# Decoder layer on one core: bf16 operands in the router's one-hot comparisons, and the softmax's subtraction of the maximum on VectorE instead of GpSimd

## What is computed

```
logits = einsum('bhqd,bhkd->bhqk', q, k) * scale
logits = logits + mask[:, None, None, :] * -1e9
attn = softmax(logits)                 # maximum subtracted, exp, divided by the sum
...
vals, idx = top_k(y @ gate_w.T, 2)
w = softmax(vals)
out = sum over the two experts e of a row:  w * W3[e](silu(W1[e] y) * (W2[e] y))
```

## Time and profile before

| what | value |
|---|---|
| three timed runs | 1579.9, 1581.67, 1582.06 us (median 1581.67) |
| the profiled execution | 1582.67 us |
| its span | 1580.8 us, so 1.87 us lie around it |
| mean granted clock of TensorE | 0.966 of 2.4 GHz |
| PE / DVE / ACT / POOL busy | 1420.2 / 1045.0 / 927.3 / 648.9 us |

### The profile page before, as it was taken

One profiled execution on the slowest core, in us unless ns is written; L12 is line 12 of the kernel. 1 busy time (PEld: TensorE's weight loads), 2 busy tenths in 40 slices (PEclk: granted clock), 3 DMA queues, 4 the chain that ended last, 5 costly groups with the idle time before them and its releaser, 6 DMA issues. The chain is left out here.

```text
span 1580.8 us, 23151 instructions
## 1 busy us (share of the span) xinstructions
PE 1420.2 (90%) x7425; PEld 902.6 (57%) x7426; DVE 1045.0 (66%) x1406; ACT 927.3 (59%) x646; POOL 648.9 (41%) x484
## 2 busy tenths in 40 slices
PE   6899999999999999999998569999984799999995
PEld 4555555555555555554554157777764566676664
DVE  7878998889888988898887726666665322222221
ACT  1879888988998899889989602222221122222221
POOL 5255456545554555455543512212220233333331
PEclk9899999999999999999999879999995899999998
DMA  4000000000000000000000313111120134233312
GB/s 145 14 1 15 27 27 13 13 27 27 13 13 27 27 13 13 27 27 13 7 14 14 113 40 109 44 42 53 46 81 14 22 87 139 35 82 81 88 30 70
DMA packets 67483, 66.90 MB, mean 42 GB/s; under 512 B 5152, under 2 KB 59936, under 8 KB 67424
## 3 DMA queue, kind: packets, MB, share of 16 engines
q1 hardware_dynamic: 60160, 56.58, 11.0%
q0 software_dynamic: 7296, 9.97, 3.8%
HBM read 48.70 MB, written 19.92 MB: 43 GB/s over the span
## 5 line engine op out<-in xcount | busy, mean ns | idle before, releaser
L1630 POOL TENSOR_TENSOR v_aug<-v_aug,wts 128x1024 f32<-128x1024 f32 x96 | 254.8, 2654 | 250.1 <-ACT wts L1483 245.5
L998 DVE TENSOR_SCALAR wts<-ps_s,k 128x1024 f32<-128x1024 f32 x240 | 297.2, 1280 | 85.4 <-PE ps_s L538 64.5
L1475 ACT ACTIVATE wts<-wts 128x4096 f32<-128x4096 f32 (+1 forms) x80 | 231.8, 2935 | 88.5 <-DVE wts L998 68.8
L553 PE MATMUL ps_o<-wts,g_r 128*64 128x512 f32 x1024 | 251.4, 614 | 11.3 <-ACT wts L1483 11.2
L1481 ACT ACTIVATE wts<-wts,eps_d 128x4096 f32<-128x4096 f32 (+1 forms) x80 | 241.5, 3019 | 0.2
L1483 ACT ACTIVATE wts<-wts 128x4096 f32<-128x4096 f32 (+1 forms) x80 | 235.1, 2939 | 2.5
L1396 DVE TENSOR_TENSOR wts<-rinv,ps_s 128x352 f32<-128x352 f32 x76 | 39.6, 521 | 253.7 <-ACT rinv L1548 170.6
L793 PE MATMUL ps_s<-wts,qk 128*128 x608 | 197.9, 469 | 3.1 <-issue 2.3
L987 DVE TENSOR_TENSOR v_aug<-v_aug,wts 128x1024 f32<-128x1024 f32 x96 | 156.1, 1626 | 5.4 <-ACT wts L1483 5.1
L538 PE MATMUL ps_s<-q_hi,k_hi 64*128 64x512 f32 x512 | 115.8, 446 | 40.3 <-DVE wts L998 30.1
L793 PEld LDWEIGHTS ps_s<-wts,qk 128*128 128x128 f32 x608 | 110.6, 192 | 64.6 <-issue 16.8
(11 more groups left out here) (240 smaller groups left out, 2425.2 us busy)
## 6 DMA issues: line engine op xcount, KB each, us to landing
wts<-in_w SPq DMA_DIRECT2D x16, 704.0 KB, 5.4
h_t<-o_raw SPq DMA_DIRECT2D x16, 512.0 KB, 2.6
qk<-h_t SPq DMA_DIRECT2D x16, 512.0 KB, 4.1
wts<-in_w SPq DMA_DIRECT2D x8, 640.0 KB, 7.1
raw_qk<-in_w_in SPq DMA_DIRECT2D x32, 128.0 KB, 2.2
raw_vg<-in_w_in SPq DMA_DIRECT2D x32, 128.0 KB, 2.2
acc<-wts SPq DMA_DIRECT2D x17, 128.0 KB, 1.7
wts<-in_x SPq DMA_DIRECT2D x2, 1024.0 KB, 6.0
```

The source lines that it names most:

```text
L553: mm = pe.matmul(ps_o[r, t], v_pair[:, b, r], wts[:, h, b, t], start=b == 0, stop=b == SB - 1)
L998: dve.tensor_scalar(wts[:, h, b, :], ps_s[:, h, :], k2[:, 2 * b + h:2 * b + h + 1], 0.0, ALU.add, ALU.max).then_inc(S_.max_ok, 1)
L1475: act.activation(chunk(start, end), chunk(start, end), ACT.Sqrt).then_inc(S_.sqrt_ok, 1)
L1630: pool.tensor_tensor(acc_w[:, 0], acc_w[:, 0], wts[:, 0, b], ALU.add).then_inc(S_.add_ok, 1)
```

## The change

The router's constants and slot numbers become bf16 (three copies of constants are made at the end of step 16 on VectorE), and the subtraction moves from GpSimd's step into VectorE's `mask_max`, behind the reduction:

```diff
-        hl_f = take(4 * NT)
+        hl_f = take(2 * NT).bitcast(BF16)
+        rb = take((P + ET + NT) // 2).bitcast(BF16)
+        pos_b, tile_b, tok_b = rb[:, 0:P], rb[:, P:P + ET], rb[:, P + ET:P + ET + NT]
@@ VectorE, mask_max
-                if n >= 1:
-                    dve.wait_ge(S_.sub_ok, i)
                 dve.tensor_reduce(lmax[:], lg, AX.X, ALU.max).then_inc(S_.lmax_ok, 1)
+                dve.wait_ge(S_.lmax_ok, i + 1)
+                dve.tensor_tensor(lg, lg, lmax[:].unsqueeze(2).broadcast_to([P, XH, KC]), ALU.subtract).then_inc(S_.sub_ok, 1)
@@ VectorE, at the end of step 16
                     dve.tensor_copy(sums, rc[:, R_TRI:R_ONES + P])
+                    dve.tensor_copy(pos_b, rc[:, R_POS:R_POS + P])
+                    dve.tensor_copy(tile_b, rc[:, R_TILE:R_TILE + ET])
+                    dve.tensor_copy(tok_b, rc[:, R_TOK:R_TOK + NT]).then_inc(S_.rb_ok, 1)
@@ VectorE, router
+            dve.wait_ge(S_.rb_ok, 1)
             dve.wait_ge(S_.hl_ok, 2)
-                q = dve.tensor_tensor(oh_hi[k][:, :, 0], rc[:, R_TILE:R_TILE + ET]...
+                q = dve.tensor_tensor(oh_hi[k][:, :, 0], tile_b...
-                dve.tensor_tensor(oh_lo[k], rc[:, R_POS:R_POS + P]...
+                dve.tensor_tensor(oh_lo[k], pos_b...
-                                  rc[:, R_TOK:R_TOK + NT].unsqueeze(2).broadcast_to([P, NT, ET]), ALU.mult)
+                                  tok_b.unsqueeze(2).broadcast_to([P, NT, ET]), ALU.mult)
@@ VectorE, weigh_slots
-                dve.tensor_tensor(one_hot, rc[:, R_TILE:R_TILE + ET]...
+                dve.tensor_tensor(one_hot, tile_b...
@@ GpSimd, step
-                if s2:
-                    pool.wait_ge(S_.lmax_ok, t)
-                    pool.tensor_tensor(lg, lg, lmax[:].unsqueeze(2).broadcast_to([P, XH, KC]), ALU.subtract).then_inc(S_.sub_ok, 1)
```

More of the change, by code:

```diff
@@ L249, in program @@
         tok_now = sb("tok_now", [P, 2], U32)
-        names = ("x_in", "xb_in", "cst_in", "c_in", "fill_s", "fill_ok", "xnb_ok", "max8_ok", "at_ok", "stats_ok", "aggr_ok", "std_ok", "rstd_ok", "xn_ok", "tr_ok", "xnt_ok",
+        names = ("x_in", "xb_in", "cst_in", "c_in", "fill_s", "fill_ok", "xnb_ok", "rb_ok", "max8_ok", "at_ok", "stats_ok", "aggr_ok", "std_ok", "rstd_ok", "xn_ok", "tr_ok", "xnt_ok",
                  "qk_in", "vg_in", "wqk_ok", "wvg_ok", "xh_ok", "x2_in", "q_proj", "k_proj", "v_proj", "g_proj", "norm_mm", "k2_mm",
@@ L260, in program @@
                  "pta_ok", "lr1", "r1_ok", "lr2", "r2_ok", "ms_ok", "lr3", "r3_ok", "exp_ok",
-                 "x1b_ok", "sub_ok", "base_ok", "top_ok", "topi_ok", "topf_ok", "dlt_ok", "pe_ok", "pw_ok", "wf_ok",
+                 "x1b_ok", "sub_ok", "base_ok", "top_ok", "topf_ok", "dlt_ok", "pe_ok", "pw_ok", "wf_ok",
                  "rc_in", "oh_ok", "a_ok", "rank_mm", "rt_ok", "tab_ok", "slot_ok", "hl_ok", "oh2_ok", "tok_mm", "tok_ok",
@@ L1328, in _ @@
             dve.tensor_copy(hl_f, hl_i[:]).then_inc(S_.hl_ok, 1)
+            dve.wait_ge(S_.rb_ok, 1)
             dve.wait_ge(S_.hl_ok, 2)
             for k in range(2):
-                q = dve.tensor_tensor(oh_hi[k][:, :, 0], rc[:, R_TILE:R_TILE + ET].unsqueeze(1).broadcast_to([P, NT, ET]),
+                q = dve.tensor_tensor(oh_hi[k][:, :, 0], tile_b.unsqueeze(1).broadcast_to([P, NT, ET]),
                                       hl_f[:, k * NT:(k + 1) * NT].unsqueeze(2).broadcast_to([P, NT, ET]), ALU.is_equal)
@@ L1334, in _ @@
             for k in range(2):
-                dve.tensor_tensor(oh_lo[k], rc[:, R_POS:R_POS + P].unsqueeze(1).broadcast_to([P, NT, P]),
+                dve.tensor_tensor(oh_lo[k], pos_b.unsqueeze(1).broadcast_to([P, NT, P]),
                                   hl_f[:, (2 + k) * NT:(3 + k) * NT].unsqueeze(2).broadcast_to([P, NT, P]), ALU.is_equal)
@@ L1364, in weigh_slots @@
                 one_hot = oh_w[k][:, 0]
-                dve.tensor_tensor(one_hot, rc[:, R_TILE:R_TILE + ET].unsqueeze(1).broadcast_to([P, NT, ET]),
+                dve.tensor_tensor(one_hot, tile_b.unsqueeze(1).broadcast_to([P, NT, ET]),
                                   hl_f[:, k * NT:(k + 1) * NT].unsqueeze(2).broadcast_to([P, NT, ET]),
@@ L1674, in _, with step @@
             pool.wait_ge(S_.c_in, C_IN)
-            def step(t, s1=True, s2=True, s4=True):
+            def step(t, s1=True, s4=True):
                 if s4:
@@ L1690, in _ @@
             for t in range(4):
-                step(t, s2=t >= 1, s4=t >= 3)
+                step(t, s4=t >= 3)
             with pool.Fori(4, NT) as t:
@@ L1694, in _ @@
             for t in range(NT, NT + 3):
-                step(t, s1=False, s2=t <= NT)
+                step(t, s1=False)
             def fetch(k, par, n):
```

## The result

The changed kernel takes 1.0151 times the time before, 95% interval [1.0129, 1.0173]. On 1581.67 us that is about 1605.6 us, where 1594.9 was forecast and 1598 was the upper end of the range. The direction was right, the size was not. Six runs lie between 1599.37 and 1630.97 us (median 1609.03), those of the kernel before beside them between 1576.57 and 1586.14: the new kernel also scatters further, by 31.6 us against 9.6, and by 11.6 without its two slowest. (Ratios here are of runs at most 1.5% above the fastest of their kernel; medians and ranges in the text are of all runs.) The profiled execution took 1603.76 us, its span is 1601.5, 20.7 longer than before.

What follows compares the result with a forecast made beforehand. It took a loop ring of VectorE (reduction to group 1's copy), then TensorE to the logits, as the bound. Terms 11.55 + 1.31 + 0.57 + 0 - 0.85 + 0.62 = 13.2 us on 1581.67 gave 1594.9 us; range 1590 to 1598 (its own 1592 to 1598).

Steps and rivals of the forecast that it cites:

- The ring: Tile loop: VectorE from the reduction to the copy of group 1, then TensorE to the logits, sets the 16.67 us period.
- VectorE's price: Subtraction in the tile loop: 1.44 us on VectorE, with the division starting 2.84 us after the reduction instead of 1.79.
- copies and comparisons: Router constants' three casts, at the end of VectorE's step 16, and its bf16 comparisons: both costed at nothing.
- 11 x 1.05 = 11.55: Steps 5 to 15 of the tile loop: division delayed by 1.05 us in each, 11.55 us in all.
- the 1.31 of step 4: Tile loop, step 4: the division follows the reduction without a wait, so it is delayed by 1.31 us.
- TensorE falls to its lower clock in the loop: Rival: about 1 us more idle ahead of `turn_o` halves the loop's clock, some 100 us, 1695 us in all; chance 0.02.
- the prediction's own signs of being wrong: Loop period staying at 16.7 us, L1335 near 1.2 us, or the loop's clock under 1.00.
- Step 1: First loop step, no division: TensorE waits 4.56 us for the exponential, which comes sooner; a gain of 0.85 us.
- Step 2: Second loop step: division 2.84 us after the reduction instead of 2.27, a loss of 0.57 us.
- Step 3: Third loop step: TensorE's 0.73 us wait for the DMA covers the delay; taken as 0, bound 0.57 us.
- Step 16: Last subtraction: VectorE delayed 1.48 us, the transposes follow `x_out`; path delayed by 0.62 us, bound 1.48.
- the rival with 3.5 us: Router: bf16 comparisons run faster, saving 3.5 us ahead of TensorE's L775, total 1591.4 us; chance 0.12.

Runs made afterwards that it cites:

- e1: The changed kernel with three extra matmuls of constants on TensorE ahead of `turn_o` in every step, against the kernel before: ratio 1.0161, median 1621.32 us.
- A alone filled: Same run as `e1`: of TensorE's three idles per step in the changed kernel, only the 1.03 us ahead of `turn_o` filled with extra matmuls; ratio 1.0161.
- f12: The kernel before (subtraction on GpSimd) with `best_two` one step later, ahead of the mask, and `h_t` loaded in two halves: ratio 0.9891, median 1564.71 us.

## Why the prediction missed

- **The ring and VectorE's price: right.** Subtraction 1.44 us, division 2.83 us after the reduction (2.84), step of 17.61 us (17.7), TensorE's idle ahead of `turn_o` 1.03 us (1), copies and comparisons worth nothing. The term "11 x 1.05 = 11.55" and the 1.31 of step 4, 12.86 together, measure 11.2 at full clock: from the copy of group 1 to the mask it is 6.92 us instead of 7.02, all of it between the start of the logits and the mask (2.75 instead of 2.85; why isn't seen), so a usual step loses 17.61 - 16.69 = 0.92 us.
- **The clock in the loop: the step that failed.** It stood as a rival, "TensorE falls to its lower clock in the loop", with the right cause (about 1 us more idle ahead of `turn_o`), but priced as all or nothing, "some 100 us in all", and so held for nearly impossible (0.02); only for step 16 did I count an earlier fall at a limited price, "1 to 2 us". The clock comes and goes within single steps, which costs 0.2 to 1.7 us in ten of twelve, 8.7 us in all in this trace, and up to 2.9 us a step in others. Without it the profiled kernel would have been 20.7 - 8.7 = 12.0 us slower, 1593.7 us on the median, inside "1592 to 1598". Its model of a fall was the tail, which stays at 0.50. The row to weigh was that of step 1 (933.07:949.30, above), with a clock of 0.89 and an idle of 4.56 us in it: a fall that lasts for part of a step. A clock under 1.00 in the loop was one of the prediction's own signs of being wrong.
- **Step 1: wrong by 0.83.** The exponential does start earlier, by 0.86 us, but the clock of this stretch went from 0.89 to 0.79, and its period stayed 16.21. In `e1`, the same program up to there, the clock was 1.00 and the period 13.72, so the clock weighed more here than the term.
- **Step 2: +0.26 instead of +0.57.** `turn_x` comes 0.54 us later, but the output projection behind it had waited about 0.2 us for `h_t`, and this wait took up the difference.
- **Step 3: +0.15**, with a clock of 0.90 where it was 1.00.
- **Step 16: -0.07 instead of +0.62.** Group 0 and 1 do start 1.59 us later (6.67 us after the reduction, against 5.08 in the earlier trace rows), but the clock comes back during them: groups 2 and 3 take 0.64 and 0.66 us instead of 1.97 together.
- **The comparisons: right**, against the rival with 3.5 us. With one operand broadcast along the innermost dimension the bf16 form takes as long as the f32 form (2284 ns against 2287 for 2048 elements), as L1370 had shown. That the broadcast is the reason no run here isolates, since none has a bf16 comparison in which both operands move.
- **Small slips in the sums.** "Slower by more" adds up to 0.91 and "same" to 0.04, where 0.90 and 0.05 stand; a usual period before was 16.69 us, and the 16.67 is the mean with step 4's 16.50. Neither changes the forecast.
- **The scatter was not foreseen.** Why the clock falls in one step and not in the next with the same idles is open; that the same kernel gave 1.0151 and 1.0124 shows no difference between chips, since the intervals overlap.

## What to carry to other kernels

Ask of a move between engines which engine's order is the ring: here 2.25 us on GpSimd lay off it and 1.44 us on VectorE lay on it, and the piece worth moving was another one, the small instructions of `best_two`, out of VectorE's ring into its wait. Where a delay opens idles of about a microsecond in a busy TensorE loop, price a clock that falls for parts of single steps, and count it by how long it lasts and where the slow matmuls land: beside another engine's work it cost 0.2 to 1.1 us in the changed kernel, on the ring 1.6 to 2.9. Filling only some of the idles gave no gain here (1.0161 and 1.017), and four of six runs with A alone filled took over 1620 us.

## What the runs showed of the hardware

- TensorE's granted clock fell at idles of 0.7 to 1.8 us in the midst of work, and came back within the same step: behind 1058.73 transposes took 1.91 us instead of 1.04, and the query at 1067.34 took 1.14 again. The Trainium skill, "TensorE: Matmul & The Clock Gate", section "HAM oscillation — how this bites in real kernels", ties such falls to long waits for DMA between bursts of matmuls, of which this loop has none; by that the changed kernel would have kept its clock and taken 1593.7 us. The trace disagrees: 10 falls in 12 steps, and none once the idles were filled. The same page of the Trainium skill, section "A second HAM failure mode: psum-queue depth-cycling", speaks of short idles that are frequent enough to switch the clock, which is nearer to what is seen.
- The 8-element copy of the earlier trace rows took 0.60 us beside GpSimd's L1691 (1027.09, GpSimd from 1026.93 to 1027.66). With `best_two` moved away from GpSimd's work it took 171 ns in all 16 steps of `f12`, so the work beside it was worth about 0.4 us (0.60 - 0.17) of each loop step's VectorE time.
